# Low-rank attention: where the small products, the query product and one row product stand in each head's block

## The reference

```python
# low-rank attention, B, S = (4, 256) is only unpacked; shapes follow h_t (8, 1024, 128), 8 heads
c_q = h_t @ W_DQ + b_DQ
c_kv = h_t @ W_DKV + b_DKV
q_c = (c_q @ W_UQ + b_UQ).reshape(b, s, N_HEADS, D_K).transpose(0, 2, 1, 3)
k_c = (c_kv @ W_UK + b_UK).reshape(b, s, N_HEADS, D_K).transpose(0, 2, 1, 3)
v_c = (c_kv @ W_UV + b_UV).reshape(b, s, N_HEADS, D_K).transpose(0, 2, 1, 3)
...
scores = jnp.einsum('bhsd,bhtd->bhst', q, k) * scale
attn = jax.nn.softmax(scores, axis=-1)
o = jnp.einsum('bhst,bhtd->bhsd', attn, v_c)
...
return o @ W_O + b_O
# around it
x = x + _L1_attn_ref(_layernorm(x, axis=-1), ...)
x = x + 0.5 * _L1_ffn_ref(_layernorm(x, axis=-1), L1_ffn_weight, L1_ffn_bias)
```

## Time and profile before

| | before |
|---|---|
| time, median of 3 runs | 1764.55 us (1761.39 to 1765.56) |
| the profiled execution, time | 1760.61 us |
| its span | 1757.4 us |
| PE busy | 1570.5 us (89%) |
| DVE busy | 1281.2 us (73%) |
| ACT busy | 1054.1 us (60%) |
| POOL busy | 1016.5 us (58%) |

### The profile page before, as it was taken

One profiled execution on the slowest core, in us unless ns is written; L12 is line 12 of the kernel. 1 busy time (PEld: TensorE's weight loads), 2 busy tenths in 40 slices (PEclk: granted clock), 3 DMA queues, 4 the chain that ended last, 5 costly groups with the idle time before them and its releaser, 6 DMA issues.

```text
span 1757.4 us, 42514 instructions
## 1 busy us (share of the span) xinstructions
PE 1570.5 (89%) x16971; PEld 1079.2 (61%) x16971; DVE 1281.2 (73%) x2345; ACT 1054.1 (60%) x1670; POOL 1016.5 (58%) x727
## 2 busy tenths in 40 slices
PE   4679999999877899998998999999899899999995
PEld 4557777777775555665665665566566566556554
DVE  5647777777598587786786877787787678687862
ACT  5447777777677266566555646565655655565662
POOL 5300011110056297787877788777887787777782
PEclk9879999999988599999999999999999999999998
DMA  4566656666000000000001001001001000100101
GB/s 127 126 147 153 168 145 157 156 159 155 3 28 1 1 8 11 8 11 8 11 8 22 8 11 20 8 10 20 10 8 23 7 9 10 20 10 10 21 11 31
DMA packets 198681, 81.63 MB, mean 46 GB/s; under 512 B 152552, under 2 KB 177492, under 8 KB 198356
## 3 DMA queue, kind: packets, MB, share of 16 engines
q1 hardware_dynamic: 198484, 78.93, 20.1%
HBM read 39.79 MB, written 29.88 MB: 40 GB/s over the span
## 4 chain that ended last, share of the span: by engine, by line
PE 29%; DVE 20%; issue 11%; POOL 5%; ACT 2%; SPq 0%; DMA 0%; DVEq 0%; POOLq 0%; ACTq 0%
DVE amax L1880 19%; PE pair L1994 13%; PE pair L1988 6%; PE pair L1941 3%; POOL Wm L1967 2%; PE pair L1687 2%; PE pair L1870 1%; PE pair L1729 1%; PE pair L1701 1%; PE pair L1716 1%; POOL Wm L1841 1%; POOL rstd L532 1%; ACT key_high L1755 1%; PE pair L1723 0%; PE pair L1694 0%
## 5 line engine op out<-in xcount | busy, mean ns | idle before, releaser
L1954 ACT ACTIVATE prob<-pair 128x1024 f32<-128x1024 f32 x512 | 523.2, 1025 | 338.3 <-PE pair L1941 298.0
L1880 DVE TENSOR_REDUCE amax<-pair 128x2 f32<-128x1024 f32 x512 | 585.6, 1216 | 62.5 <-PE pair L1870 61.4
L1967 POOL TENSOR_TENSOR w_mix<-w_mix,prob 128x1024 f32<-128x1024 f32 x128 | 305.1, 2384 | 74.0 <-ACT prob L1954 66.3
L1967 POOL TENSOR_TENSOR Wm<-Wm,prob 128x1024 f32<-128x1024 f32 x124 | 295.7, 2385 | 34.3 <-ACT prob L1954 27.1
L1870 PE MATMUL pair<-key_high,q_hi 64*128 64x512 f32 x1024 | 223.8, 449 | 40.7 <-DVE amax L1880 25.7
L530 POOL TENSOR_SCALAR veps<-mv 128x8 f32<-128x8 f32 x47 | 11.4, 243 | 418.0 <-DVE mv L503 416.1
L1994 PE MATMUL pair<-prob,values 128*32 128x256 f32 x4096 | 237.9, 384 | 0.0
L1196 DVE TENSOR_REDUCE mx_neg<-pair 128x4 f32<-128x512 f32 x256 | 164.7, 686 | 90.2 <-PE pair L1100 89.5
L1941 PE MATMUL pair<-q_hi,key_low 64*128 64x512 f32 x1024 | 204.3, 393 | 0.0
L1870 PEld LDWEIGHTS pair<-key_high,q_hi 64*128 64x128 f32 x1024 | 99.2, 189 | 159.1 <-DVE amax L1880 111.3
L1994 PEld LDWEIGHTS pair<-prob,values 128*32 128x32 f32 x4096 | 139.7, 112 | 88.1 <-issue 5.4
(11 more groups left out here) (229 smaller groups left out, 2628.6 us busy)
## 6 DMA issues: line engine op xcount, KB each, us to landing
rows_mem<-once SPq DMA_DIRECT2D x128, 128.0 KB, 2.0
queries<-rows_mem SPq DMA_DIRECT2D x64, 256.0 KB, 4.5
keys<-rows_mem SPq DMA_DIRECT2D x16, 1024.0 KB, 7.0
rows_mem<-once SPq DMA_DIRECT2D x128, 64.0 KB, 1.9
q_shift<-shift_cols SPq DMA_DIRECT2D x512, 0.5 KB, 2.0
yT<-o_norm SPq DMA_DIRECT2D x256, 32.0 KB, 1.8
x<-x_dram SPq DMA_DIRECT2D x8, 512.0 KB, 7.3
out_dram<-x SPq DMA_DIRECT2D x7, 512.0 KB, 3.4
```

What stands on the lines that cost most here:

```text
L1880: e.tensor_reduce(amax1[:, u % 2].rearrange("p (s t) k -> p s t k", s=2)[:, :, t, half], pair[places_m["row", r][0]][:, :].rearrange("p (s ...
L1954: e.activation(prob1[:, g % P_BUFS, :], pair[g % 2][:, :], ACT.Exp, scale=SCALE1).then_inc(*key_exp.up(g))
L1967: e.tensor_tensor(into, into, p, ALU.add).then_inc(*summed_keys.up(g))
```

## The change

It does four things in the block, and leaves the number of products of each kind as it was.

1. The query product and the items share one pair: the query product takes one bank of it, the first item the other; the second item goes into the query product's bank once `q_low` was made from it. So the block itself has two uses of the pairs where it had three (two in block 7), and a row product is a third.
2. The items are spread: 0 `quant` (two), 1 `proj` first half, 2 `proj` second half, 3 `turn` (two), 4 `low` first half and `product` first half, 5 `low` and `product` second halves, 6 `const` and `diff` first half, 7 `value` and `diff` second half.
3. PE's order in a block is: key scores, query product, first item, totals, second item, a row product (`EARLY_ROWS` has all eight heads), weighing. Step 4 has one row product. DVE's order is: `q_low`, first item, norm work, `o_inv`, second item, row maximum, `o_norm`. The first half of a block's pair is thus read by DVE ahead of `o_inv`, the second half behind it.
4. The norm work "d" moves a block later where it stood together with "m" (`d stats` to block 3, `d aggregate` to 4), its tiles are scaled by ACT in one go in block 5, ACT does norm work behind the items, and SP stores a finished batch five blocks later.

The diff, cut to its core:

```diff
-NORM_WORK = (("m stats", None), ("m aggregate", None), ("m tiles", "d stats"), (None, "d aggregate"),
-             (None, "d first tiles"), (None, "d last tiles"), (None, "d scales"), (None, "d rounding"))
-def rows_at(g):
-
-    r = g + ROW_LEAD
-    return {BURST: [], BURST + 1: [r - 1, r]}.get(g % NT, [r])
+EARLY_ROWS = range(NH)
+NORM_WORK = (("m stats", None), ("m aggregate", None), ("m tiles", None), (None, "d stats"),
+             (None, "d aggregate"), (None, "d tiles"), (None, "d scales"), (None, "d rounding"))
...
-        kind, a = {0: ("quant", b - 2), 1: ("proj", b - 1), 2: ("product", b - 2), 3: ("turn", b + 1),
-                   4: ("low", b + 1), 5: ("diff", b + 1), 6: ("value", b + 1)}.get(h, (None, 0))
-        if kind is None or not 0 <= a < B or b == B and h:
-            return []
-        return [("const", a, 0), ("value", a, 0)] if kind == "value" else [(kind, a, i) for i in range(2)]
+        items = {0: (("quant", b - 2, 0), ("quant", b - 2, 1)), 1: (("proj", b - 1, 0),), 2: (("proj", b - 1, 1),),
+                 3: (("turn", b + 1, 0), ("turn", b + 1, 1)), 4: (("low", b + 1, 0), ("product", b - 2, 0)),
+                 5: (("low", b + 1, 1), ("product", b - 2, 1)), 6: (("const", b + 1, 0), ("diff", b + 1, 0)),
+                 7: (("value", b + 1, 0), ("diff", b + 1, 1))}[h]
+        return [item for item in items if 0 <= item[1] < B and (b < B or h == 0)]
...
-        if query is not None:
-            use(("query", query), [("query", query, 0)])
+        if query is not None or items:
+            use(("items", g), ([("query", query, 0)] if query is not None else []) + items)
         if weigh is not None:
             use(("weigh", weigh), [("weigh", weigh, 0)])
-        if items:
-            use(("items", g), items)
+        if row is not None:
+            use(("row", row), [("row", row, 0)])
...
+        def item_bank(g, n):
+
+            return 2 * places_m["items", g][0] + 1 - n
...
-                for r in rows:
-                    pe_row_scores(e, r)
+                if query is not None or items:
+                    pair_free(e, ("items", g))
                 if query is not None:
-                    pair_free(e, ("query", query))
-                    pe_low_part(e, ("query", query, 0), 2 * places_m["query", query][0])
+                    pe_low_part(e, ("query", query, 0), item_bank(g, 1))
+                for n, item in enumerate(items[:1]):
+                    pe_low_part(e, item, item_bank(g, n))
+                if weigh is not None:
+                    pe_totals(e, weigh)
+                for n, item in enumerate(items[1:], start=1):
+                    if query is not None:
+                        low_bank_free(e, ("query", query, 0))
+                    pe_low_part(e, item, item_bank(g, n))
+                if row is not None and early_row(g):
+                    pe_row_scores(e, row)
                 if weigh is not None:
                     pe_weigh(e, weigh)
-                if items:
-                    pair_free(e, ("items", g))
-                for n, item in enumerate(items):
-                    pe_low_part(e, item, 2 * places_m["items", g][0] + n)
+                if row is not None and not early_row(g):
+                    pe_row_scores(e, row)
...
                 if weigh is not None:
                     dve_invert_totals(e, weigh)
-                    dve_normalise(e, weigh)
-                for n, item in enumerate(items):
-                    dve_low_part(e, item, 2 * places_m["items", g][0] + n)
+                for n, item in enumerate(items[1:], start=1):
+                    dve_low_part(e, item, item_bank(g, n))
+                if row is not None and early_row(g):
+                    dve_row_max(e, row)
+                    if row % NT == NT - 1:
+                        dve_row_top(e, row // NT)
+                if weigh is not None:
                     dve_normalise(e, weigh)
...
-                if h == 3 and 2 <= b < B:
-                    sync_store(e, b - 2)
+                if h == 0 and 3 <= b <= B:
+                    sync_store(e, b - 3)
```

More of the change, by code:

```diff
@@ L281, in low_rank_plan @@
             copies, held = held, []
-        rows = [r for r in rows_at(g) if 0 <= r < NT * U]
+        row = g + ROW_LEAD if 0 <= g + ROW_LEAD < NT * U else None
         b, n = divmod(g, NT * NH)
         final = [FINAL[n]] if b == B and n in FINAL else []
-        for r in rows:
-            use(("row", r), [("row", r, 0)])
         if g % NT == BURST:
@@ L293, in low_rank_plan @@
             items = TAIL[n]
-        if query is not None:
-            use(("query", query), [("query", query, 0)])
+        if query is not None or items:
+            use(("items", g), ([("query", query, 0)] if query is not None else []) + items)
         if weigh is not None:
             use(("weigh", weigh), [("weigh", weigh, 0)])
-        if items:
-            use(("items", g), items)
+        if row is not None:
+            use(("row", row), [("row", row, 0)])
         held = items if items else held
-        steps.append((g, features, copies, final, rows, work, query, weigh, items))
+        steps.append((g, features, copies, final, row, work, query, weigh, items))
     return opening, opening_banks, steps, places
@@ L1589, in act_norm_work @@
         def act_norm_work(e, kind, b):
[L1590 to L1595, removed]
+            if kind.endswith("tiles"):
+                norm_scale_act(e, kind[0], b, 0, NT)
             elif kind == "d rounding":
@@ L1991, in pe_weigh @@
             done.then_inc(*totalled.up(u))
-            for t, part in enumerate(tiles):
+        def pe_weigh(e, u):
+            b = u // NH
+            weighed = weigh_banks(u)[0]
+            e.wait_ge(*value_ready.at(b))
+            for t in range(NT):
+                part = prob1[:, (NT * u + t) % P_BUFS, :]
                 for q in range(4):
@@ L2054, in pe_low_rank @@
             e.wait_ge(*keys_done.at((0, 1)))
-            for g, features, copies, final, rows, work, query, weigh, items in plan_m:
+            for g, features, copies, final, row, work, query, weigh, items in plan_m:
                 if g == CONST_AT:
@@ L2098, in act_low_rank @@
                 for n, item in enumerate(items):
-                    act_low_part(e, item, 2 * places_m["items", g][0] + n)
+                    act_low_part(e, item, item_bank(g, n))
+                for kind, b in work:
+                    act_norm_work(e, kind, b)
         def dve_low_weights(e, part):
@@ L2139, in dve_low_rank @@
                     dve_final(e, part, half)
[L2140 to L2143, removed]
                 if query is not None:
-                    dve_low_part(e, ("query", query, 0), 2 * places_m["query", query][0])
+                    dve_low_part(e, ("query", query, 0), item_bank(g, 1))
+                for n, item in enumerate(items[:1]):
+                    dve_low_part(e, item, item_bank(g, n))
                 for kind, b in work:
```

22 lines of the change are left out of this document (9 added, 13 removed).

## The result

| | before | after |
|---|---|---|
| time, median of 4 runs | 1765.05 us | 1826.53 us |
| ratio to before, 95% interval | | 1.035 (1.032 to 1.038) |
| span of the profiled execution | 1757.4 us | 1824.2 us |

The change makes the kernel 61 us slower. The direction was forecast, the size was not: 1786 us with a range up to 1812.

The account below looks back on a forecast made before the run. PE was taken to bound the block, DVE's row maxima the steps outside it. Attention +7 us and clock +16 us, the rest nothing, made +23 on 1760.6: 1784, given as 1786 us; own range 1772 to 1800, eight in ten 1753 to 1812.

Parts of the forecast that it names:

- What bounds the kernel: Whole attention: no single engine; PE bounds the block, DVE's eight row maxima the steps outside it, with ACT close by.
- Where R lies: Start of the row product in each block, set by reads of the shared pair; a full batch 1.9 us longer.
- the sign of 3.5 to 4 us of idle time ahead of L1859: Blocks 4 to 6: PE would idle that long before the row product, until DVE's read of the second item.
- The price of the clock: Weighing after 16 long stalls in blocks 4 to 6: lower clock costs 1.0 us each, 16 us, bounds 0 and 21.
- The stretch behind the weighing: From the weighing's end to the next block: 8.6 us where it was 9.5, saving 0.9 us a period.
- W + 8.6: Start of the next block, with W the weighing's end; ACT's exponentials set it, DVE would allow W + 8.4.
- The faster rival: Stretch behind the weighing 8.2 us and low clock wholly inside the stalls: 1743 to 1750 us, chance 0.15.
- POOL's wait of the earlier trace: Block 4: the totals' 2.56 us wait for POOL would go, as its norm aggregate moves away from the feature steps.
- ACT's norm work and the stores: ACT behind the items, and SP's stores: both taken at nothing; without cover eight tiles on ACT would cost 3 us.
- the rival that the clock falls at each stall: Block 7 and early batches pay too, low stretches reach the seven steps behind: about 1805 us, chance 0.14.
- the one of 1.77 us of the earlier trace: A stall in the kernel before, not followed by the lower clock; stalls of 1.9 to 2.2 us were taken alike.

## Why the prediction was wrong in size

**What bounds the kernel.** Right: the blocks and the stretches behind them alternate, and every period could be put together from the two.

**Where R lies.** Right. The start of the row product was forecast at 4.0, 3.85, 3.85, 4.0, 7.55, 7.4, 7.5 and 6.4 us in blocks 0 to 7; it is 3.97, 3.88, 3.88, 3.97, 7.27, 7.52, 6.88 and 6.26 in the mean of the full batches. Block 6 was the worst, by 0.6. The stalls came out shorter than forecast, 3.2, 3.4, 3.1 and 1.6 us in blocks 4 to 7 where 3.7, 3.6, 4.0 and about 2 were given, so the sign of 3.5 to 4 us of idle time ahead of L1859 was not met.

**The price of the clock.** This is the step that failed: "I take 1.0 of 1.29 for each, 16 us, bounds 0 and 21". The mechanism was right (each of the 16 stalls of 3.1 to 3.4 us is followed by the lower clock), the size was off. The bound of 1.29 came from one row, a weighing of which the first half had the lower level. I took it for the most that a fall costs, and a part of the low stretch for free because it would lie in the stall. Neither holds. At ten of the 16 places the low stretch lasts 3.4 us, as in the earlier trace rows, but at seven of these it starts less than 0.2 us ahead of the weighing or inside it, and over the ten the weighing is 1.5 us longer in the mean. At the other six, blocks 4 and 6 of the batch above among them, it lasts 6.8 us and covers the weighing almost whole: 6.04 to 6.33 us in place of 3.66, and the row product ahead of it holds the queue for 0.72 us in place of 0.43. A safer upper bound stood in the same rows: if a clock of 0.50 doubles the whole weighing, that is 3.6 us, an estimate, and times 16 it is 58. Measured: 37 us by filling the stall (34 by the attention of the profiled executions); the weighings of the trace add up to 33 of it. With 37 in place of 16 the forecast moves from 1786 to 1807.

**The stretch behind the weighing.** Forecast W + 8.6, measured W + 8.8, and 0.43 for the row product, not 0.34. Over 62 periods these are 13 and 6 us. Part of it is in the working: its terms, 1.07, 7.5 and 0.2, add up to 8.8, and it went on with 8.6. I also took a couple of exponentials for 2.15 us; they start 2.19 apart, and 2.4 where the tiles with a fourth term begin. ACT in the timeline behind block 4:

```profile
1132.49 1.94 ACT L1943 ACTIVATE prob<-pair 128x1024 f32<-128x1024 f32 x2 [11.98 <-PE pair L1930]
1134.68 1.96 ACT L1943 ACTIVATE prob<-pair 128x1024 f32<-128x1024 f32 x2 [0.25 <-PE pair L1930]
1137.11 4.35 ACT L1943 ACTIVATE prob<-pair 128x1024 f32<-128x1024 f32 x4 [0.47 <-PE pair L1930]
```

ACT waits for PE's key scores between the couples, and PE's scores wait for the exponential two back. This loop is the bound there now, not DVE. The faster rival, which needed 8.5 or less, is out.

**Sum.** 23 us forecast; 21 for the clock, 19 for the stretch and the row product, and less 5 for R make 58, against 59 measured in the attention. Either miss alone would have left the time below the 1812 of the range; the two together did not.

**The other steps.** POOL's wait of the earlier trace rows is gone, as forecast, and the move of the norm work that takes it away is worth 24 us alone. ACT's norm work and the stores are hidden: none of the eleven longest waits of the batch names them. Block 7 and the early batches: the rival that the clock falls at each stall holds only in part. Of the seven stalls of 1.6 us in block 7 one was followed by a low stretch, of the two of 2.0 us in batches 0 and 1 one. The prediction had put beside this rival the rule of the Trainium skill ("TensorE: Matmul & The Clock Gate", HAM oscillation). The loop that this section describes waits some 3 to 5 us in each turn, and the stalls here of 3.1 to 3.4 us agree with it, 16 of 16; that the stalls of block 7 would pay too was the prediction's own step, not the section's.

**What the length of the stall does not tell.** In the batches of the attention all stalls of 2.5 us and more were followed by the lower clock. Below that it is open: stalls of 2.0 us were in five of six cases over all runs, those of 1.62 in two of five, and the one of 1.77 us of the earlier trace rows, which the prediction took as harmless, never in the kernel before (seven cases) but in four of eight with the norm work moved. The prediction also says that the rows show a fall for the 2.56 us stall alone. The kernel before had another, in block 6 of four batches, where PE stood still for no longer than 0.21 us in the 8 us ahead of it. It had done the weighing and the narrow products `const` and `value` there. The stretch ahead and the low one, columns as in the earlier trace rows:

```profile
1138.90:1142.40 3.50, 3.50 (x38) 3.05 (x32) 1.76 (x4) 0.00 (x0) 3.50 (x2) 1.00 0.13 1
1142.40:1145.80 3.40, 3.40 (x18) 2.42 (x20) 1.86 (x3) 1.02 (x1) 1.07 (x2) 0.50 0.15 39
```

Block 6 took 19.0 to 19.3 us in these batches and 18.2 in the two full ones without it, so it is in the 143.5 us of the prediction's batch and does not change its sum. But the clock was seen to fall without a stall too, and no run here shows what decides it.

## What to carry to other kernels

Before putting a product into a bank that other work must leave first, look at what stands behind it in the same queue: here 3.6 us of weighing waited for a read that had itself nothing to do with it, and behind the weighing the same product found its pair free in seven blocks of eight. A stall on TensorE is to be priced twice, with its own length and with the products behind it at the lower clock, and the second part can be the larger one (a stall of 1.62 us, then a weighing 1.68 us longer, where the clock fell). When several edits come together, time each alone: of the changes that came together here, moving the norm work was a gain of 24 us, and moving one row product ahead of the weighing a loss of 136.

## What the hardware showed that was not expected

Adding 96 useless products a batch made the kernel 37 us faster; it is a test for the clock that needs no other change.

DVE's `d_scale` (128 by 32, one multiply and one maximum) takes 0.18 us in the kernel with the norm work behind the reads, and 1.68 us with it ahead of them and the row product behind the weighing. In the second, a POOL addition runs from 1098.78 to 1101.15 and `d_scale` ends 0.05 us behind it. The first row is of the former, the other two of the latter:

```profile
1107.47 0.18 DVE L1559 TENSOR_SCALAR d_scale<-d_amax 128x32 f32<-128x32 f32 x1
```

```profile
1099.52 1.68 DVE L1559 TENSOR_SCALAR d_scale<-d_amax 128x32 f32<-128x32 f32 x1
```

```profile
1098.78 2.37 POOL L1956 TENSOR_TENSOR w_mix<-w_mix,prob 128x1024 f32<-128x1024 f32 x1
```

It is no single case. Over the ten profiles `d_scale` runs 90 times. 49 of these took 0.27 to 2.30 us, and each of them started while a POOL addition of 128 by 1024 was under way and ended 0.04 us behind its end; the other 41 took 0.17 or 0.18. It looks as if DVE had waited for POOL's access to SBUF. The ends fit that in all 49 cases; no run was made to test it.
